# Weighting and adding the experts' rows on GpSimd instead of VectorE in the second attention stage

## The reference, cut to what matters

```
x = x + L0_ffn(layernorm(x))        # top-2 experts + a shared expert
x = x + L1_attn(layernorm(x))       # 16 heads of 8 features, 256 tokens, ALiBi bias
...
q, k, v = split(x_normed @ qkv_w.T + qkv_b)
scores  = q @ k.T / sqrt(8) - |i - j| * slope[head]
out     = softmax(scores) @ v
return out @ out_w.T + out_b
```

## Time and profile before

| what | value |
|---|---|
| time, median of 3 runs | 1744.41 us (1743.11 to 1745.42) |
| profiled execution: its time | 1735.23 us |
| its span | 1733.4 us |
| PE busy | 1519.8 us (88%) |
| DVE busy | 1165.6 us (67%) |
| ACT busy | 992.3 us (57%) |
| POOL busy | 493.9 us (28%) |
| second attention stage | about 1007 to 1408 us of the span |

### The profile page before, as it was taken

The page is one execution under the profiler, slowest core; times in us unless marked ns, Lnnn a source line. Parts: engine busy times, 40 slices in busy tenths (PEclk is TensorE's granted clock), DMA queues, the critical chain, the costliest instruction groups (busy, mean ns, idle before and its releaser), DMA issues. The chain is left out here.

```text
span 1733.4 us, 38581 instructions
## 1 busy us (share of the span) xinstructions
PE 1519.8 (88%) x11126; PEld 1090.1 (63%) x11127; DVE 1165.6 (67%) x3687; ACT 992.3 (57%) x2564; POOL 493.9 (28%) x736
## 2 busy tenths in 40 slices
PE   7999999999999776459999948999999868887798
PEld 4777777777776564238888835555555535555497
DVE  5776777677767375755666637777777728994465
ACT  5776777677767344106666626666666625553254
POOL 3222222222222243443333222222222012221033
PEclk9999999999999876669999969999999979997899
DMA  6000000000000300001111110000000000000000
GB/s 198 2 0 0 0 0 0 0 0 0 0 0 1 146 25 25 1 5 42 42 46 42 37 49 12 12 12 12 12 12 12 1 1 1 0 0 1 1 25 25
DMA packets 34214, 34.67 MB, mean 20 GB/s; under 512 B 5744, under 2 KB 29936, under 8 KB 33392
## 3 DMA queue, kind: packets, MB, share of 16 engines
q1 hardware_dynamic: 29808, 25.08, 4.5%
q0 software_dynamic: 4352, 8.92, 2.1%
HBM read 25.07 MB, written 8.91 MB: 20 GB/s over the span
## 5 line engine op out<-in xcount | busy, mean ns | idle before, releaser
L556 POOL TENSOR_SCALAR a_prob<-a_prob,a_inv 128x128 f32<-128x128 f32 (+1 forms) x256 | 127.0, 507 | 387.6 <-DVE a_inv L468 387.6
L414 ACT ACTIVATE a_prob<-a_psS,a_low 128x128 f32<-128x128 f32 (+1 forms) x512 | 210.5, 438 | 0.6 <-DVE a_low L458 0.6
L458 DVE CUSTOM_DVE_ANT_0 a_psS<-a_psS,a_bias 128x128 f32<-128x128 f32 (+1 forms) x512 | 167.6, 389 | 56.2 <-PE a_psS L295 39.4
L1590 ACT ACTIVATE a_probT<-a_psZ 128x512 f32<-128x512 f32 x256 | 138.9, 594 | 75.6 <-PE a_psZ L1402 75.6
L405 ACT COPY a_probT<-a_psT 128x384 f32<-128x384 f32 x256 | 123.5, 482 | 96.2 <-PE a_psT L336 94.1
L1663 DVE TENSOR_REDUCE a_low<-a_psS 128x4 f32<-128x1024 f32 x128 | 156.2, 1221 | 26.9 <-PE a_psS L1402 24.6
L336 PE MATMUL a_psT<-ident,a_prob 128*128 128x128 f32 x768 | 133.2, 282 | 2.8 <-ACT a_probT L405 2.7
L336 PEld LDWEIGHTS a_psT<-ident,a_prob 128*128 128x128 f32 x768 | 88.0, 140 | 60.2 <-issue 48.6
L295 PE MATMUL a_psS<-a_qk 64*128 64x128 f32 (+1 forms) x1024 | 120.0, 353 | 1.3 <-ACT a_qk L397 0.9
L1196 POOL DMA_INDIRECT e_rows<-rows_dram,source x72 | 68.2, 948 | 160.8 <-PE e_psX L1230 136.9
L414 ACT ACTIVATION_READ_ACCUMULATOR a_prob<-a_psS,a_low 128x1 f32 x512 | 113.8, 222 | 0.0
(11 more groups left out here) (301 smaller groups left out, 3928.8 us busy)
## 6 DMA issues: line engine op xcount, KB each, us to landing
sorted_out<-e_y SPq DMA_DIRECT2D x72, 64.0 KB, 1.5
in_lo<-in_gate_up SPq DMA_DIRECT2D x4, 1024.0 KB, 9.3
x<-in_x SPq DMA_DIRECT2D x8, 256.0 KB, 6.8
down<-in_down SPq DMA_DIRECT2D x1, 2048.0 KB, 16.7
rows_dram<-rows SPq DMA_DIRECT2D x8, 256.0 KB, 2.3
out<-x SPq DMA_DIRECT2D x8, 256.0 KB, 2.3
e_rows<-rows_dram,source POOLq DMA_INDIRECT x72, 2.7
a_sel_in<-in_sel SPq DMA_DIRECT2D x1, 1024.0 KB, 4.8
```

The source lines that it names most:

```text
L414: nc.scalar.activation(prob[:, 2 * (p % 4) + k, lo:hi], psS[:, u, lo:hi], ACT.Exp, bias=low[:, u, i:i + 1], scale=-1.0, accum_out=total[:, ...
L458: nc.vector.tensor_tensor_reduce(psS[:, u, lo:hi], psS[:, u, lo:hi], bias0[:, 2 * p + k, lo:hi], 1.0, LEAST, ALU.add, ALU.min, low[:, u, i ...
L556: nc.gpsimd.tensor_scalar(w, w, inv[:, 2 * (q % 2) + 1, i:i + 1], 1.0, ALU.mult, ALU.mult).then_inc(norm_done[1], 1)
L1590: nc.scalar.activation(probT[:, (p + half + 1) % 2, 2 * half + c, :, :].rearrange("p j s -> p (j s)"), psZ[:, c, :], ACT.Exp, scale=-1.0). ...
```

## The change

VectorE's `add_choice` goes. GpSimd's `hand_over(b)`, which only signalled that the rows had landed, now does the work for a batch: four `tensor_scalar` that weight the four 128 x 128 pieces of `back` in place, then two `tensor_tensor` of 128 x 256 that add the first and the second choice into `g.x`, each behind a wait for the instructions before it. `statistics(b)` on VectorE waits for the last add.

```diff
@@ layer1_attention, VectorE
-            def add_choice(b, k):
-                if k == 0:
-                    dve.wait_ge(gathered, b + 1)
-                else:
-                    dve.wait_ge(added, b * 2 * BT + BT)
-                dve.sem_inc(dve_seen, 1)
-                for t in range(BT):
-                    row = bass.ds(b * BT + t, 1)
-                    v.scalar_tensor_tensor(out=g.x[:, row, :], in0=back[:, row, k, :], scalar=g.weight[:, k, row],
-                                           in1=g.x[:, row, :], op0=ALU.mult, op1=ALU.add).then_inc(added, 1)
             def statistics(b):
-                dve.wait_ge(added, b * 2 * BT + 2 * BT)
+                dve.wait_ge(added, b + 1)
...
-                add_choice(0, 0)
-                add_choice(0, 1)
                 statistics(0)
...
-                    if prep and p == 0:
-                        add_choice(b + 1, 0)
-                        add_choice(b + 1, 1)
@@ layer1_attention, GpSimd
             def hand_over(b):
                 pool.wait_ge(fetched[b % 4], 16 * 2 * BT * (b // 4 + 1))
-                pool.sem_inc(gathered, 1)
+                for t in range(b * BT, b * BT + BT):
+                    for k in range(2):
+                        nc.gpsimd.tensor_scalar(back[:, t, k, :], back[:, t, k, :], g.weight[:, k, t:t + 1], 1.0, ALU.mult,
+                                                ALU.mult).then_inc(weighted, 1)
+                pool.wait_ge(weighted, 2 * BT * (b + 1))
+                rows = slice(b * BT, (b + 1) * BT)
+                nc.gpsimd.tensor_tensor(g.x[:, rows, :], g.x[:, rows, :], back[:, rows, 0, :], ALU.add).then_inc(first_added, 1)
+                pool.wait_ge(first_added, b + 1)
+                nc.gpsimd.tensor_tensor(g.x[:, rows, :], g.x[:, rows, :], back[:, rows, 1, :], ALU.add).then_inc(added, 1)
                 ln_in.rstd(pool, b)
```

More of the change, by code:

```diff
@@ L1351, in layer1_attention @@
         fetched = [ph.sem(f"fetched{i}") for i in range(4)]
-        gathered = ph.sem("gathered")
+        weighted = ph.sem("weighted")
+        first_added = ph.sem("first_added")
         added = ph.sem("added")
```

## The result

The changed kernel takes 1750.29 us (median of 20 runs) and the kernel before, run beside it, 1744.41 us (20 runs): ratio 1.0038, 95% interval 1.0027 to 1.0048. It is 0.4% slower, 5.9 us, where 8.3 us were forecast. Two later groups of runs, each with both kernels on one chip, give 1.0032 (1.0019 to 1.0046) and 1.0030 (1.0017 to 1.0044).

What follows compares the result with a forecast made beforehand. It took a chain between PE and DVE, neither full, to set the round. Start +4.1, meeting +4.0 in 13 rounds, rounds 0 and 1 +0.2: +8.3 us on 1744.41, so 1752.7 us; range 1744.8 to 1762.5.

Steps and rivals of the forecast that it cites:

- The start of the stage: Batch 0, where nothing covers GpSimd's six new instructions and VectorE's statistics follow them: +4.1 us once, up to +4.8.
- rival 2: Steady rounds: weighting over 0.45 us each, so adds miss VectorE's L131 pair; 1745.5 us, no change; chance 0.25.
- The gain of the adds that leave VectorE: Steady round: without the adds VectorE's reduction starts sooner and PE gains 0.27 us, not the 1.42 removed.
- rival 3: Steady rounds: VectorE is the bound and the whole 1.42 us comes back in 14 rounds; 1729 us; chance 0.08.
- Who meets whom: Rounds 2 to 14: GpSimd's first add holds VectorE's second L131, so the pair ends at 1120.45 instead of 1120.04.
- POOL TENSOR_SCALARs seem not to do this: GpSimd's TENSOR_SCALARs don't hold VectorE's; claimed from 256 L472 beside L556 that never exceed 0.349 us.
- Rival 1: Steady rounds: more of VectorE's rows held, by TENSOR_SCALARs or both adds; +0.44 to +1.1 a round, 1754 to 1763; chance 0.22.
- What the meeting costs: Rounds 2 to 14: the held L131 costs +0.31 us a round net of the gain, +4.0 us in 13 rounds.
- So the slot's second reduction starts ... 0.42 later: In the slot where the pair is held, VectorE's second reduction starts at 1120.49 instead of 1120.07.
- PE's L1475 follows a reduction's start by 1.45 us when PE is waiting: Distance read at 1137.40 to 1138.86, putting PE's instruction after the delayed reduction at 1121.94 instead of 1121.36.
- Rounds 0 and 1: GpSimd's second add near L1658 in round 0, +0.3, less 0.1 for missing adds in round 1: +0.2 us.
- double hold: VectorE held until the first add, then until the second: 1.24 us delay, +1.1 a round, +19 in all.

Runs made afterwards that it cites:

- kernel whose adds wait: Changed kernel plus one wait: from batch 3 on GpSimd's adds start only behind VectorE's ln.apply pair; 1747.10 us, ratio 1.0004 to before.
- weights twice: Changed kernel with GpSimd's four weighting TENSOR_SCALARs issued twice, so the adds come later (other values); 1729.91 us, ratio 1.0014 to before.
- both edits: Changed kernel with batch 0 back on VectorE and, from batch 3, GpSimd's adds behind VectorE's ln.apply; 1726.32 us (0.9992), then 1724.81 us (0.9979).
- three weights: Changed kernel with the last of a batch's four weightings left out from batch 3 on; 1739.46 us, ratio 1.0065 to before.
- no fetches: Changed kernel without the four fetch DMAs of batches 2 to 15, rows of batch 0 or 1 reused; 1740.94 us, ratio 1.0075 to before.
- third profile: Changed kernel run a third time, unchanged, on a chip without the late results; 1733.71 us against 1727.96 before, ratio 1.0030.

## Why the prediction was right, point by point

**The start of the stage: +4.1 us. Shown.** From the first fetch to PE's L139: 11.51 us before, 15.60 to 15.62 in every kernel with the changed kernel's six instructions there, 11.51 to 11.62 with batch 0 on VectorE. The prices held too: TENSOR_SCALAR 0.355 (0.37 forecast), adds 0.72 (0.74). For the 0.37 that is in part luck. It came from the difference between a distance of starts, 0.58, and a duration, 0.476; the two durations in the rows, 0.512 and 0.476, would have given 0.44, at the edge of rival 2.

**The gain of the adds that leave VectorE: -0.27 us a round. Shown.** 22.20 against 22.46 once nothing meets. The other 1.16 us of the 1.42 were never on the path, so rival 3 is out. Rival 2 (they miss each other) is the kernel whose adds wait, and gives in its rounds what was forecast for it.

**Who meets whom. Shown for the changed kernel; one reason given for it was wrong.** The pair of L131 takes 1.01 to 1.02 us with the second one held (1.01 by the prediction's times). But "POOL TENSOR_SCALARs seem not to do this" is wrong: the kernel with weights twice shows L131 held by them, to 0.08 behind their ends. The L472 rows could not show it. There L556 of GpSimd comes in behind VectorE, 0.17 us into the first L472, and the one that waits is L556, with 0.537 us in place of the 0.36 of the same form in the changed kernel. So the rule that the prediction cites from the Trainium skill ("SBUF — State Buffer", the section on ports), which covers any instruction of GpSimd, agrees with the trace for both operations, save that recorded starts less than 0.1 us apart don't tell which came first. In the changed kernel the weightings cost VectorE nothing because the last of them is over at 1127.42, 0.03 us after the first L131 starts, and that one takes its usual 0.35. Rival 1 had its first condition right and its price wrong.

**What the meeting costs: +0.31 us net a round. This term was mis-sized; it is 0.02.** Two steps of it failed. "So the slot's second reduction starts ... 0.42 later" took the growth of the pair for the delay of what follows. Before the change that reduction waited for TensorE's scores, whose last piece ends at 1120.04, 0.03 ahead of it, just as the pair does:

```profile
1119.77 0.27 PE L1402 MATMUL a_psS<-slopes,distance 128*128 128x256 bf16 x1
```

A held pair lets it start 0.07 to 0.08 before the pair's recorded end (1142.55 against 1142.62). So it is 0.94 behind the pair's start where it was 0.63: 0.31 late, 0.11 less than forecast. And "PE's L1475 follows a reduction's start by 1.45 us when PE is waiting" was read in another slot, at 1137.40. In this slot it is 1.27 (1142.55 to 1143.82); before it was 1.29 there as well (1120.07 to 1121.36), a row that was on the table. That is 0.18 less. 0.31 - 0.11 - 0.18 = 0.02, which is what a round shows. Five lengths of the pair give the price of a hold directly:

| pair of L131 | round, us | kernel |
|---|---|---|
| 0.60 | 22.20 | both edits |
| 0.66 | 22.20 | weights twice |
| 1.02 | 22.48 | changed |
| 1.39 | 22.86 | three weights |
| 1.70 | 23.16 | no fetches |

Each 0.1 us of the pair beyond about 0.73 costs a round 0.1 us; the 0.73 is an estimate from these rows, and fits the two numbers above (the scores let the reduction start at 0.65, the pair 0.08 before its end). Rival 1 would thus have cost 0.38 to 0.69 a round over the changed kernel, and its threshold was nearer than "within 0.1 us of both": 0.03. In round 2 of the changed kernel's third profile it did occur (pair 1.57, round 23.21); in the first profile it did not (1.02).

**Rounds 0 and 1: +0.2 us. Open.** The meeting with L1658 (L1647 now) in round 0 is in the first profile after, where it takes 0.74 in place of 0.69 us and GpSimd's second add 1.05 in place of 0.73; in the third profile they miss each other. From PE's L139 to the first `ln.rstd` two profiles of one kernel (both edits) have 53.62 and 55.00 us; that scatter is larger than the term.

**The sum.** 4.1 + 13 x 0.02 = 4.4 us, and 0.7 more where round 2 falls into the double hold: 4.4 to 5.1, against the 5.3 to 5.9 measured in three groups of runs, whose intervals reach down to 2.9 us. The forecast of 8.3 had the sign, the place and the mechanism of this kernel; it was above because of the term of the meeting, and its wrong belief about GpSimd's TENSOR_SCALARs did no harm only because the last of them is over in time.

## What to carry to other kernels

When work moves from VectorE to GpSimd, the amount says little: look for the places where a long instruction of GpSimd (here an add of 0.72 us) comes in beside VectorE's TENSOR_SCALARs from SBUF to SBUF, fix the order there with a wait, and leave work that nothing covers where it is (here the two made a gain of 0.2% out of a loss of 0.3%). Read the distance between two engines in the slot in question, not in a like one, and a delay from the start of the next instruction, not from the end of the held one. When two engines never meet in one of the two possible orders, the rows say nothing about the other order. And take a second profile of the kernel before, on another chip if possible, before a difference of 1% between two profiles is explained.

## What the hardware showed that was not expected

The late results belong neither to the change nor to a kernel. Both the kernel before and the changed one have profiles with them (rounds of 23.65 and 23.70 to 23.82 us) and without them (22.46 and 22.48). All four profiles of the first group of experiments, on one chip, have them, all eight of the two later groups, on two other chips, have not, and the median of the kernel before is 1746.75 us in the first group and 1727.46 and 1727.96 in the others. Of the 19 us 14 rounds of 1.2 are 17; the rest is open. In the rows TensorE's instructions start on time at a granted clock of 1.00, and the engines that wait for what they wrote go on some 2 us later. The wait always stands beside the four fetches, but no kernel without fetches ran on a chip that shows it, so it stays open whether they have a part. That the chip decides is what these runs suggest; no chip was used twice.

A hold between the two engines works both ways and instruction by instruction: the add that came in 0.11 us behind VectorE's L131 took 0.82 us in place of 0.72, and of two L131 each waited for one add, never for two. A held L131 ends 0.08 to 0.09 us behind the instruction that held it, whichever operation that was; this distance shows a hold even where the time it costs, 0.06 us, looks like none.
